# Probability tiles through memory in one fetch each, 24 of 36, with y in the order of rows 4 i + a

## What is computed

```python
def _L0_attn_ref(x, Wq, Wk, Wv, Wo, q_norm_w, k_norm_w):
    q = (x @ Wq.T).reshape(b, s, H, HD).transpose(0, 2, 1, 3)      # k, v alike, 8 heads
    q = _rmsnorm(q, q_norm_w); k = _rmsnorm(k, k_norm_w)
    scores = jnp.einsum('bkgqd,bksd->bkgqs', qg, k) / math.sqrt(HD)
    bias = jnp.where(rel > 0, NEG_INF, slopes[:, :, None, None] * rel)
    attn = jax.nn.softmax(scores + bias[None], axis=-1)
    out = jnp.einsum('bkgqs,bksd->bkgqd', attn, v)
    return out.transpose(...).reshape(b, s, H * HD) @ Wo.T
def _L0_ffn_ref(x, A, B, Wr, br):
    scores = H * softmax(einsum('bsd,hd->bsh', x, Wr) + br)
    return SCALING * einsum('bshr,hor,bsh->bso', einsum('bsd,hrd->bshr', x, A), B, scores)
x = x + attn(layernorm(x)); x = x + ffn(layernorm(x))
```

## Time and profile before

| | |
|---|---|
| median of 3 runs | 2056.68 us (2056.5 to 2058.53) |
| profiled execution | 2058.6 us, span 2056.5 us, granted clock 0.997 |
| busy: TensorE, weight loads | 1993.2 us (97%), 1698.1 us |
| busy: VectorE, ScalarE, POOL | 1363.5, 1162.6, 1189.2 us |
| DMA | 283.81 MB in 896141 packets, 677721 of them under 512 B |

### The profile page before, as it was taken

One profiled execution on the slowest core, in us unless ns is written; L12 is line 12 of the kernel. 1 busy time (PEld: TensorE's weight loads), 2 busy tenths in 40 slices (PEclk: granted clock), 3 DMA queues, 4 the chain that ended last, 5 costly groups with the idle time before them and its releaser, 6 DMA issues.

```text
span 2056.5 us, 33589 instructions
## 1 busy us (share of the span) xinstructions
PE 1993.2 (97%) x10956; PEld 1698.1 (83%) x10956; DVE 1363.5 (66%) x3431; ACT 1162.6 (57%) x3314; POOL 1189.2 (58%) x1188
## 2 busy tenths in 40 slices
PE   7999999999999999999999899999999999999996
PEld 6888888888888888888888788787878878788774
DVE  6667667666666666768876566565666656566696
ACT  4656656565665656655555465555656555465552
POOL 3574645647465574655645557465664746657473
PEclk9999999999999999999999999999999999999998
DMA  4573855657466573765635637365463745637254
GB/s 164 138 161 119 192 141 150 132 154 166 129 171 145 136 159 113 181 181 142 135 109 141 142 96 173 96 154 139 123 124 108 172 101 137 161 81 165 69 122 99
DMA packets 896141, 283.81 MB, mean 138 GB/s; under 512 B 677721, under 2 KB 839513, under 8 KB 895969
## 3 DMA queue, kind: packets, MB, share of 16 engines
q1 hardware_dynamic: 844064, 179.44, 41.7%
q10 hardware_dynamic: 51904, 102.24, 14.2%
HBM read 152.59 MB, written 128.97 MB: 137 GB/s over the span
## 4 chain that ended last, share of the span: by engine, by line
PE 76%; SPq 8%; DMA 4%; DVE 4%; issue 4%; POOL 2%; ACT 2%; DVEq 0%; POOLq 0%; ACTq 0%
PE s_ps L1106 16%; PE q_ps L1106 15%; PE y_ps L1106 14%; PE o_ps L1106 14%; PE turn_ps L1193 9%; SPq L653 7%; PE turn_ps L1106 7%; DMA p_bounce<-probs_odd 2%; POOL probs_odd L881 1%; DMA p_raw_b<-p_bounce 1%; DMA p_bounce<-probs_even 1%; DVE oT_lo L1029 1%; PE turn_ps L1187 1%; SPq L642 1%; ACT oT_hi L823 1%
## 5 line engine op out<-in xcount | busy, mean ns | idle before, releaser
L881 POOL TENSOR_TENSOR probs_odd<-probs_odd,p_inv 128x256 f32<-128x256 f32 (+3 forms) x256 | 318.0, 1257 | 180.1 <-DVE p_inv L1008 179.2
L881 POOL TENSOR_TENSOR probs_even<-probs_even,p_inv 128x128 f32<-128x128 f32 (+3 forms) x256 | 261.3, 1043 | 191.3 <-DVE p_inv L1008 190.5
L1106 PE MATMUL s_ps<-kT_hi,qT_hi 128*128 128x512 f32 (+3 forms) x768 | 272.5, 355 | 4.1 <-DVE neg_max L1001 3.8
L1001 DVE CUSTOM_DVE_ANT_0 probs_odd<-s_ps,rel 128x256 f32<-128x256 f32 (+3 forms) x256 | 209.3, 820 | 97.3 <-issue 96.6
L802 ACT ACTIVATE probs_odd<-probs_odd,neg_max 128x256 f32<-128x256 f32 (+3 forms) x256 | 212.2, 831 | 91.7 <-DVE neg_max L1001 91.6
L1106 PE MATMUL s_ps<-kT_hi,qT_lo 128*128 128x512 f32 (+3 forms) x768 | 262.4, 342 | 0.0
L1106 PE MATMUL s_ps<-kT_lo,qT_hi 128*128 128x512 f32 (+3 forms) x768 | 261.7, 341 | 0.0
L802 ACT ACTIVATE probs_even<-probs_even,neg_max 128x128 f32<-128x128 f32 (+3 forms) x256 | 185.1, 725 | 118.7 <-DVE neg_max L1001 118.4
L1001 DVE CUSTOM_DVE_ANT_0 probs_even<-s_ps,rel 128x128 f32<-128x128 f32 (+3 forms) x256 | 174.9, 687 | 109.8 <-issue 108.8
L987 DVE STREAM_TRANSPOSE p_raw<-p_raw 128x512 f32<-128x512 f32 x252 | 174.9, 700 | 83.5 <-DMA p_raw<-p_bounce 83.2
L1106 PE MATMUL q_ps<-wqT_hi,xnT_hi 128*128 128x512 f32 x512 | 217.2, 424 | 1.0 <-DVE qn L1012 0.8
(11 more groups left out here) (131 smaller groups left out, 5068.3 us busy)
## 6 DMA issues: line engine op xcount, KB each, us to landing
p_raw<-p_bounce SPq DMA_DIRECT2D x1008, 64.0 KB, 2.3
p_bounce<-probs_odd SPq DMA_DIRECT2D x60, 384.0 KB, 3.1
p_raw_b<-p_bounce SPq DMA_DIRECT2D x256, 64.0 KB, 2.4
p_bounce<-probs_odd SPq DMA_DIRECT2D x60, 256.0 KB, 2.8
p_bounce<-probs_even SPq DMA_DIRECT2D x60, 256.0 KB, 3.0
p_bounce<-probs_even SPq DMA_DIRECT2D x64, 192.0 KB, 2.4
wq_kept<-wqT_hi ACTq DMA_DIRECT2D x8, 1024.0 KB, 4.5
wq_kept<-wqT_lo ACTq DMA_DIRECT2D x8, 1024.0 KB, 6.8
```

The lines of the kernel that those rows point to most:

```text
L881: nc.gpsimd.tensor_tensor(row, row, p_inv[:, s % 2, h:h + 1].to_broadcast((P, L)), ALU.mult).then_inc(sems["normalise"], 1)
L1001: nc.vector.tensor_tensor_reduce(out=probs[s % 2][:, h, 0:L], in0=s_ps[:, at_col:at_col + L], in1=rel[:, S - L:S], scale=-float(slopes[w % ...
L1106: last = nc.tensor.matmul(target, a, m, start=start and i == 0 and k == 0, stop=stop and i == len(pairs) - 1 and k == 2)
```

## The change

More tiles go through memory: 24 of 36 in all groups but the eighth, which keeps 16. A tile comes back in one DMA: the send now writes pieces of 32 numbers (128 B) in an order that lets the fetch read pieces of 128 numbers (512 B) into all 128 partitions at once. That order puts the 128 queries of a block as 32 a + i for row 4 i + a. So that both kinds of tiles agree, TensorE's transposes of p write their columns in the same order, with a step in PSUM; `o`, `y` and the rest of the layer's second half then have rows in that order, and y is loaded and stored by four DMAs for each block of 128 rows (for the first sequence two on SP and two on ScalarE's queue). x of the first sequence is normalised from y, so its transposes put the columns back in natural order, again with a step in PSUM. The lists of order are new throughout; of them only the end of `GROUP_A` is shown.

```diff
-MEMORY_TILES = ({2: (2,), 3: (2, 3), 4: (2, 3, 4), 5: (2, 3, 4, 5), 6: (3, 4, 5, 6), 7: (2, 3, 4, 5, 6, 7)},
+MEMORY_TILES = ({2: (1, 2), 3: (1, 2, 3), 4: (2, 3, 4), 5: (2, 3, 4, 5), 6: (2, 3, 4, 5, 6), 7: (1, 2, 3, 4, 5, 6, 7)},
                 {2: (2,), 3: (2, 3), 4: (3, 4), 5: (3, 4, 5), 6: (4, 5, 6), 7: (3, 4, 5, 6, 7)},
-                {2: (2,), 3: (2, 3), 4: (2, 3, 4), 5: (2, 3, 4, 5), 6: (3, 4, 5, 6), 7: (2, 3, 4, 5, 6, 7)})
+                {2: (1, 2), 3: (1, 2, 3), 4: (2, 3, 4), 5: (2, 3, 4, 5), 6: (2, 3, 4, 5, 6), 7: (1, 2, 3, 4, 5, 6, 7)})
 PROLOGUE = (
-    "load_y.2 load_y.0 load_y.1 load_y.3 load_y.7 x_stats.2 load_y.4 x_stats.0 load_y.6 x_stats.1 load_wkv.first "
-    "x_stats.3 x_stats.7 load_wq.first x_moments.1 x_stats.4 x_rstd.1 x_moments.0 x_rstd.0 x_norm.1 x_moments.7 "
+    "load_y.1 load_y.0 load_y.4 load_y.3 load_wkv.first x_stats.1 x_stats.0 load_y.2 x_moments.1 x_moments.0 "
...
 GROUP_A = (
...
+    "high.kv.1 lower_p.6.3 send_p.7.3 lower_p.6.4 flip_p.6.5 fetch_p.6.6 norm_q.8 values.6.1 high.kv.2 low.kv.1 y.5 "
+    "fetch_p.7.1 upper_p.6.5 lower_p.6.5 flip_p.6.6 fetch_p.7.2 low.kv.2 values.6.2 flip_p.7.1 turn.p.7.0 upper_p.6.6 "
+    "add_y.5 values.6.3 lower_p.6.6 turn.q.8 upper_p.7.1 values.6.4 high.p.7.0 lower_p.7.1 values.6.5 fetch_p.7.3 "
+    "low.p.7.0 values.6.6 flip_p.7.2 fetch_p.7.4 turn.kv.3 o_high.6 high.q.8 o_low.6 upper_p.7.2 flip_p.7.3 "
+    "lower_p.7.2 low.q.8 upper_p.7.3 q.9.0 flip_p.7.4 lower_p.7.3 fetch_p.7.5 values.7.0 upper_p.7.4 high.kv.3 "
+    "values.7.1 lower_p.7.4 fetch_p.7.6 y.6 low.kv.3 inv_k fetch_p.7.7 flip_p.7.5 upper_p.7.5 flip_p.7.6 values.7.2 "
+    "lower_p.7.5 values.7.3 upper_p.7.6 flip_p.7.7 q.9.1 lower_p.7.6 norm_k upper_p.7.7 values.7.4 q.9.2 lower_p.7.7 "
+    "q.9.3 add_y.6 values.7.5 square_q.9 values.7.6 values.7.7 inv_q.9 turn.k.0 o_high.7 turn.k.1 high.k.0 o_low.7 "
...
+        def rows_in_order(columns):
+            return columns.rearrange("p (a i) -> p i a", a=NBLK)
...
-        p_bounce = nc.dram_tensor("p_bounce", [2, NT, G, P, P], F32).ap()
+        p_bounce = nc.dram_tensor("p_bounce", [2, G, NT, NBLK, P, BLOCK], F32).ap()
...
+            x_by_y = x.rearrange("b (t i a) d -> b t a i d", i=BLOCK, a=NBLK)
+            out_by_y = out.rearrange("b (t i a) d -> b t a i d", i=BLOCK, a=NBLK)
...
-                sp.dma_start(p_bounce[s % 2, first:s + 1, h].rearrange("u p c -> p u c"),
-                             probs[s % 2][:, h, first * P:(s + 1) * P].rearrange("p (u c) -> p u c", c=P)).then_inc(p_sent[s % 2], 16)
+                sp.dma_start(p_bounce[s % 2, h, first:s + 1].rearrange("u b p j -> p (u b) j"),
+                             probs[s % 2][:, h, first * P:(s + 1) * P].rearrange("p (u j) -> p u j", j=BLOCK)).then_inc(p_sent[s % 2], 16)
...
-                blocks = p_bounce[s % 2, j].rearrange("h (a i) (b j) -> b i (h a) j", i=BLOCK, j=BLOCK)
-                for b in range(NBLK):
-                    sp.dma_start(raw_p(n)[b * BLOCK:(b + 1) * BLOCK, :].rearrange("p (n j) -> p n j", j=BLOCK),
-                                 blocks[b]).then_inc(p_fetched[n], 16)
+                tile = p_bounce[s % 2, :, j].rearrange("h b (i a) j -> (b i) h (a j)", a=NBLK)
+                sp.dma_start(raw_p(n).rearrange("p (h k) -> p h k", h=G), tile).then_inc(p_fetched[n], 16)
...
-                sp.dma_start(y[:, t, :], x_v[b, :, t, :]).then_inc(y_loaded[t], 16)
+                for a in range(NBLK if b else NBLK // 2):
+                    sp.dma_start(y[a * BLOCK:(a + 1) * BLOCK, t, :], x_by_y[b, t, a]).then_inc(y_loaded[t], 16)
...
-                sp.dma_start(out_v[b, :, t, :], y[:, t, :]).then_inc(stored[t], 16)
+                for a in range(NBLK):
+                    sp.dma_start(out_by_y[b, t, a], y[a * BLOCK:(a + 1) * BLOCK, t, :]).then_inc(stored[t], 16)
...
+            def load_y(w, t):
+                if w < 0:
+                    for a in range(NBLK // 2, NBLK):
+                        nc.scalar.dma_start(y[a * BLOCK:(a + 1) * BLOCK, t, :], x_by_y[0, t, a]).then_inc(y_loaded[t], 16)
...
-                    last = nc.tensor.transpose(bank[0:width, i * rows:(i + 1) * rows], source, ident[0:rows, 0:rows])
+                    columns = bank[:, i * P:(i + 1) * P]
+                    if of == "p":
+                        last = nc.tensor.matmul(rows_in_order(columns), source,
+                                                ident[:].rearrange("p (i a) -> p i a", a=NBLK), is_transpose=True)
+                    elif of == "x" and ln_batch(w) == 0:
+
+                        last = nc.tensor.matmul(columns.rearrange("p (i a) -> p a i", a=NBLK), source,
+                                                ident[:].rearrange("p (a i) -> p a i", a=NBLK), is_transpose=True)
+                    else:
+                        last = nc.tensor.transpose(bank[0:width, i * rows:(i + 1) * rows], source, ident[0:rows, 0:rows])
```

More of the change, by code:

```diff
@@ L614, in _ @@
             x_v = x.rearrange("b (t p) d -> b p t d", p=P)
-            out_v = out.rearrange("b (t p) d -> b p t d", p=P)
+            x_by_y = x.rearrange("b (t i a) d -> b t a i d", i=BLOCK, a=NBLK)
+            out_by_y = out.rearrange("b (t i a) d -> b t a i d", i=BLOCK, a=NBLK)
             def load_wkv(w, *first):
@@ L658, in load_y @@
                 if b:
-                    sp.wait_ge(stored[t], 16)
-                sp.dma_start(y[:, t, :], x_v[b, :, t, :]).then_inc(y_loaded[t], 16)
+                    sp.wait_ge(stored[t], 16 * NBLK)
+                for a in range(NBLK if b else NBLK // 2):
+                    sp.dma_start(y[a * BLOCK:(a + 1) * BLOCK, t, :], x_by_y[b, t, a]).then_inc(y_loaded[t], 16)
             def load_x(w, t):
@@ L690, in _ @@
             for t in range(NT):
-                sp.wait_ge(stored[t], 16 * NB)
+                sp.wait_ge(stored[t], 16 * NBLK * NB)
         @block.scalar
         def _(act):
+            x_by_y = x.rearrange("b (t i a) d -> b t a i d", i=BLOCK, a=NBLK)
+            def load_y(w, t):
+                if w < 0:
+                    for a in range(NBLK // 2, NBLK):
+                        nc.scalar.dma_start(y[a * BLOCK:(a + 1) * BLOCK, t, :], x_by_y[0, t, a]).then_inc(y_loaded[t], 16)
             def load_wkv(w, *first):
@@ L833, in sort_b @@
                 nc.scalar.activation(b_sorted.rearrange("p o h r -> p h o r"), b_raw, ACT.Copy).then_inc(sems["sort_b"], 1)
-            follow({"load_wkv": load_wkv, "load_wq": load_wq, "load_wo": load_wo, "keep_wkv": keep_wkv, "keep_wq": keep_wq,
+            follow({"load_y": load_y, "load_wkv": load_wkv, "load_wq": load_wq, "load_wo": load_wo, "keep_wkv": keep_wkv, "keep_wq": keep_wq,
                     "keep_wo": keep_wo, "back_wkv": back_wkv, "back_wq": back_wq, "back_wo": back_wo, "high": high, "upper_p": upper_p, "exp": exp, "square_q": square_q, "v_high": v_high,
@@ L905, in x_stats @@
                 b = ln_batch(w)
-                dve.wait_ge((x_loaded if b else y_loaded)[t], 16)
+                dve.wait_ge((x_loaded if b else y_loaded)[t], 16 if b else 16 * NBLK)
                 nc.vector.bn_stats(x_stat[:, t, :], x_source(b, t)).then_inc(sems["x_stats"], 1)
@@ L984, in flip_p @@
             def flip_p(w, s, j):
-                dve.wait_ge(p_fetched[raw_tile[w, s, j]], 16 * NBLK * raw_uses[w, s, j])
+                dve.wait_ge(p_fetched[raw_tile[w, s, j]], 16 * raw_uses[w, s, j])
                 raw = raw_p(raw_tile[w, s, j])
@@ L1032, in add_y @@
             def add_y(w, s):
-                dve.wait_ge(y_loaded[s], 16 * (w // NG + 1))
+                dve.wait_ge(y_loaded[s], 16 * NBLK * (w // NG + 1))
                 after(dve, "y", w, s)
```

## The result

The changed kernel takes 2101.91 us (median of 4 runs, 2099.83 to 2103.45), the kernel before on the same chip 2057.61 (4 runs): 1.0209 times as long, interval 1.0196 to 1.0222. Forecast were 2039 us, and 2025 to 2074.

The account below looks back on a forecast made before the run. TensorE, busy 1993.2 of 2056.5 us, was taken to bound the kernel. Turns -26.4, stepped outputs 0, new waits +8, start -1, last store +1.4 sum to -18 us: 2039 us from 2056.7, range 2025 to 2074.

Parts of the forecast that it names:

- the turns: TensorE, fifteen groups: 60 tiles no longer turned, four transposes or 0.44 us each, -26.4 us.
- the stepped outputs at 0: TensorE's 832 remaining transposes: writing columns with a step in PSUM costs nothing, 0 us; upper end +102 us.
- Rivals A and B: Whole kernel: stepped transpose outputs at half rate, about 2055 us, chance 0.15; at quarter rate or worse, about 2141, chance 0.09.
- the price of a small write: DMA engines: a 128 B write taken at the read's 12.6 ns, above at twice that.
- rival C: Sends of s = 7: small writes dear, deciding from about 18 ns a packet; at 25 ns 2174 us; chance 0.16.
- C's sign: Group's end: DMA share near 1, with `values` waiting for `lower_p` and `flip_p` for a DMA.
- the last store: End of the kernel: four store issues instead of one on SP, nothing left to hide them, +1.4 us.
- the term of +8 us for new waits: Group ends, over fifteen groups: tiles of s = 7 just in time, +8 us, bounds -10 and +26.
- the last send lands 1.5 us later: Group's end, s = 7: longer sends delay the first tile 1.5 us, held by its 3.1 us of slack.
- Rival D: Group's end: gain eaten by waits of 1.2 to 1.8 us a group, 2049 to 2058 us; chance 0.12.
- the start, -1: Start of the kernel: statistics of two tiles come first instead of five, -1 us, within -2 and +2.
- theory 1: Experiments' theory for 24 early tiles: their place, not their number, costs; 2021 to 2040 us forecast.

Follow-up runs that it names:

- e1: Changed kernel with all sends in 512 B pieces again instead of 128 B, fetched values scrambled, same work: 2029.87 us, 0.9875 of the kernel before.
- e5: Changed kernel with only the four sends of s = 7 back in 512 B pieces, their values wrong: 2038.63 us, 0.9908 of the kernel before.
- e3: Changed kernel's new layout with the tables and lists of the kernel before (20 tiles): 2047.44 us, 0.9962 of the kernel before.
- e14: e3 with sends of s = 7 that take tile 7.1 along, which nobody fetches: 2065.30 us, 1.0042 of the kernel before.
- e2: Changed kernel with the last fetches of s = 6 ahead of sends of s = 7 in the lists: 2130.01 us, 1.0354 of the kernel before.
- e10: Changed kernel with the four sends of s = 7 issued from ScalarE's queue instead of SP's: 2098.18 us, 1.0203 of the kernel before.
- e6: e3 with two more early tiles through memory, 2.1 and 3.1 (22 tiles): 2039.30 us, 0.9910 of the kernel before.

## Why the prediction was wrong

**Right: the turns.** 60 x 0.44 us. The chain of the kernel after still has four transposes at 0.44 us:

```profile
601.33 0.44 PE turn_ps L1211 x4
```

and e1, with the same 60 turns gone and the large pieces of before in its sends, is 25.8 us faster than the kernel before, with a later start in it. As its fetches are quicker than before too, it bears the price out but does not prove it.

**Right: the stepped outputs at 0.** The row above is of transposes that write with a step of 32 words; they last as long as those of before. Rivals A and B are out. The rule of the Trainium skill ("SBUF — State Buffer", DMA port swizzle) that any non-contiguous pattern in PSUM slows matmuls significantly is not borne out by these transposes.

**Right: the price of a small write.** 11.9 ns against the 12.6 taken, far from the 18 from which rival C would decide. By the rule of the Trainium skill ("DMA: Bandwidth & Descriptors", Specifications) pieces below 512 B are read, modified and written. These rows do not show a price for that, as writes of 128 B cost no more than reads of 128 B. C's sign, a DMA share near 1 with `values` waiting for `lower_p`, was seen all the same: the sends decide not by a dear packet but by leaving together.

**Right, nearly: the last store.** From TensorE's last matmul to the end of the span are 4.2 us and were 3.2: +1.0, where +1.4 was taken.

**Wrong: the term of +8 us for new waits.** It failed at this step: "the last send lands 1.5 us later", set against "3.1 us of slack". Four things were wrong in it.
- It charged one send with its longer time, as if the sends still left apart. In the new order three of them leave together, behind a fetch that waits for a raw tile. Then the difference counts about three times: 3.4 us on SP (5.97 against 2.33, and gaps), and 0.9 on the landing behind them.
- It looked for the victim in s = 7, at its first and its last tile. The victim is the last tile of s = 6, whose fetch is issued behind these sends. Rival D named that place, "a send that is twice as long stands ahead of the fetches of s = 6", and sized it at 1.2 to 1.8 us a group; it was 3.3 to 4.7 in the first batch.
- It gave the fetch 2.3 us to land, the row of a quarter of a tile (64 KB). A whole tile in one DMA (256 KB) lands in 3.3 us in the median, and the one that TensorE waits for in 6.08.
- It had no price for what a wait does to the clock. A stretch at half clock followed each long wait: 22.5 us, about half of what the idle time brought.

The terms as they came out: -26.4 for the turns, +46.7 of idle time, +22.5 at the lower clock (this one by subtraction; the trace gives 23); together the 42.8 us between the spans, 2056.5 and 2099.3. e5, in which the sends of s = 7 are large, took 2038.63 us, and 2039 was forecast: that is luck in part, since the start alone came out 5 us off.

**Wrong, smaller: the start, -1.** TensorE began at 7.2 us, 2.9 earlier, then waited 4.2 and 1.7 us for weights whose fetches now stand among twice as many of x; its list of the start ended at 43.6 us in place of 39.3. e3 has the same loss (43.3) with the old order, so the split of the fetches of x is enough for it, without the new list.

**What stays open.** That small sends of s = 7 are needed for most of the loss (e5) and, in the second batch and the old order, make a part of it by themselves (e14) is shown, and that neither SP's order (e2) nor its queue (e10) is all of it. The path was followed in the first batch; the smaller waits of the second in the changed kernel, of up to 3.7 us ahead of `y`, also go in e5, but their chain was not followed. How the rest of tile 7.1's price divides between its fetch, its flip and its split was not tried one by one. Nor is it settled whether 24 early tiles could be had without waits: both kernels with them had waits of their own, at POOL and at the three raw tiles of the first batch, in orders made by hand. So in these two kernels the number of tiles in a group counts too, and not the place alone as theory 1 had it. The best of the kernels whose tiles hold the right values is e6, new layout, old order, 22 tiles: 0.9910 of the time before.

## What to carry to other kernels

When a transfer becomes longer, charge it as often as such transfers can leave back to back, and look for the victim behind them in the queue, not only among their own readers: here a price per packet that was right to 6% gave a wait that was three times too small. Here a wait of 4 us of the engine that is 97% busy cost half as much again through the time at half clock behind it. And try the layout, the table and the order one by one: the same layout gains with 20 tiles or with two early ones more, loses with one late tile more, and the same 22 tiles differ by 12.5 us between the two orders.

## What the runs showed of the hardware

- Writes of 128 B from SBUF to DRAM cost the DMA engines no more than reads of 128 B: 11.9 ns by elapsed time (after, 653 to 658) against 12.6 by the share.
- Issuing is not a fixed price: a send of 3584 packets kept SP for 2.0 and 2.5 us behind another one, and for 0.61 where the one at 640.11 left alone; three of 896 packets took 2.33 us together in e5, and a send of 768 before 0.43 to 0.49.
- The granted clock fell to its lower level behind each of the seven waits of 3.3 to 4.7 us in the first batch, for 3.4 or 6.8 us. In the kernel before, a wait of 3.0 us at 1153 and those of up to 1.8 us ahead of `values` and `y` left it at the upper one.
